# Experts of a mixture layer with the weights as stationary operand, and one slot less

## The chip, the cores and the metric

The kernel runs on one core of one Trainium2 chip. It is one program of about 45,000 executed instructions. The metric is the device time in microseconds of one execution. A core has five engines: TensorE (PE: products, with PEld its weight loads and PEldq its sequencer, which works through registers, waits and branches and passes the products on), VectorE (DVE), ScalarE (ACT), GpSimd (POOL) and SyncE (SP), which issues DMAs. In a product one operand is stationary: it is loaded into the array first, 128 columns of it here. The other one moves through the array column by column.

## The reference, cut to what matters

Four sublayers follow each other: cross attention, a feed-forward layer with quantised products, a second cross attention, and a mixture of experts. The change touches the last one alone.

```python
# x: (8, 512, 512), 4096 tokens of 512 numbers; 8 experts, 2 for each token; MOE_DIM = 1024
x_flat = x.reshape(b * s, d)                       # the normed x
topk_logits, topk_idx = jax.lax.top_k(x_flat @ moe_router, 2)
topk_weights = softmax(topk_logits)
sort_idx = argsort(topk_idx.reshape(tokens * 2))   # the 8192 pairs by expert
x_sort = x_flat[token_ids_sort]
w13_out = ragged_dot(x_sort, moe_w13, group_sizes)         # (8192, 2048)
gate, up = split(w13_out, [1024], axis=-1)
hidden = silu(gate) * up
out_dispatch = ragged_dot(hidden, moe_w2, group_sizes)     # (8192, 512)
out_flat = zeros.at[token_ids_sort].add(out_dispatch * w_sort[:, None])
```

## The kernel before, in words

The stages run one after another, each a block with a barrier at its end: context, attention 0, feed-forward, attention 1, routing, experts, combine. Routing sorts the 8192 pairs of token and expert by expert into `sorted_x`, in slots of 128 rows; each slot belongs to one expert, and the number of its expert stands in `plan.expert`. There are 64 + 8 = 72 slots (`SLOTS`).

The function `experts` works through the slots. The weights of two experts at a time are held in the on-chip memory, `weights13` (gate and up, 512 x 2048) and `weights2` (1024 x 512), each as a high and a low part in bf16. A product of two numbers is made of three bf16 products (`PRODUCTS`: high with high, high with low, low with high). The stages of a slot are:

- SP loads 128 rows of `sorted_x` into `x_rows`.
- `flip_x` (line 1779): TensorE transposes them in 8 pieces, ScalarE copies the result to `x_t`.
- `half_products` (line 1789): gate and up, 512 columns of each in one half. The tokens of `x_t` are stationary, the weights move, 512 columns to a product. The result has a token in each row. Each half has 2 parts x 4 k x 3 = 24 products. Which of the two weight buffers is read depends on `expert % 2`, a value in a register; in the listing of the instructions a row `ISA` before a product is the arithmetic on registers that works out such an address.
- ScalarE applies Silu to gate (line 1849), VectorE multiplies with up (1876) and splits the product `mid` into a high and a low part, `mid_parts` (1880, 1882).
- `flip_mid` (line 1799): TensorE transposes the parts of a half in 8 pieces, and VectorE copies them to `mid_t` (1889), since the next product needs the features of `mid` in the rows.
- `output` (line 1809): `mid_t` is stationary, `weights2` moves: 8 x 3 = 24 products of 512 columns into one bank, `out`. ScalarE copies it to `y_rows` (1855), SP stores it to `sorted_y`.

Each engine goes through the slots by itself in the order written in its own `slot` function, and semaphores hold them together. `slots` writes out the first two and the last two slots and has a loop over pairs of slots between. On TensorE the order within slot s is: read the number of the expert, first half of s, transposes of the x rows of s + 1, transposes of the second half of s - 1, second half of s, output of s - 1, transposes of the first half of s. GpSimd loads the weights of the expert after next and splits them as soon as the output of the last slot of an expert is there (`pool.wait_ge(out_ready, end)`).

Of the kernel before, what the change touches and what calls it, by code (L numbers as in the profile page):

```python
# [26 lines left out]
P = 128  # L27
# [1302 lines left out]
SLOTS = (2 * B * S) // P + EXPERTS  # L1330
# [329 lines left out]
def experts(nc, core, plan, w, sorted_x, sorted_y):  # L1660
# [5 lines left out]
    with ExitStack() as stack:  # L1666
# [7 lines left out]
        mid_parts = sb("mid_parts", [P, 2, 2, 512], BF16)  # L1674
        mid_t = sb("mid_t", [P, 2, MC, P], BF16)
# [9 lines left out]
        split = sem("split"); mid_high = sem("mid_high"); mid_low = sem("mid_low")  # L1685
        x_in = [sem(f"x_in{i}") for i in range(2)]
# [4 lines left out]
        mid_flipped = sem("mid_flipped"); mid_copied = sem("mid_copied")  # L1691
# [5 lines left out]
        def slots(engine, slot):  # L1697
# [6 lines left out]
            slot(SLOTS - 2, 0, False, False)  # L1704
            slot(SLOTS - 1, 1, False, True)
# [49 lines left out]
        def _(sp):  # L1755
# [14 lines left out]
            for u in range(2):  # L1770
                sp.wait_ge(y_out[u], 16 * PAIRS)

        @block.tensor
        def _(pe):
# [20 lines left out]
            def flip_mid(s, half):  # L1795
                pe.wait_ge(mid_low, 2 * s + half + 1)
                at_least(pe, mid_copied, 2 * s + half - 1)
                for j in range(MC):
                    last = nc.tensor.transpose(mid_flip[half][:, j * P:(j + 1) * P],  # L1799
                                               mid_parts[:, half, j // 4, j % 4 * P:(j % 4 + 1) * P],  # L1800
                                               core.ident_bf[:, :])
# [206 lines left out]
```

## Time and profile before

| | |
|---|---|
| runs | 3473.69, 3482.69, 3483.56 us |
| median | 3482.69 us |
| span of the profiled execution | 3475.7 us |
| experts stage in it | 2152 to 3377 us |
| slots, time of one in the loop | 72, 16.88 us |

The profile page sums the busy time of each engine and cuts the span into 40 slices of 87 us. Each digit is the busy share of a slice in tenths. The trace answers closer questions: stretches, groups by source line, and instructions in order of time. A matmul is recorded from its start until its result is written, longer than the distance to the next one, since they are pipelined. Distances are therefore read from starts.

### The profile page before, as it was taken

The page shows a single profiled execution, that of the slowest core. Times are in us where ns is not written, and L with a number is a line of the kernel's source. Part 1 is how long each engine was busy: PE and PEld are TensorE (multiplying, and loading weights), DVE is VectorE, ACT ScalarE, POOL GpSimd, SP SyncE. Part 2 cuts the span into 40 slices and gives each one's busy share as a digit, 9 for nine tenths or more (in the row PEclk, how much of TensorE's full clock was granted, in tenths as well). Part 3 has the DMA queues.
Part 4 walks back from the last instruction along what each step waited for, and adds up shares of the span by engine and source line. Part 5 has one row for each costly group of instructions (what it writes and reads, how often), then busy time and mean ns, then how long its engine had stood idle before and what let it go on. Part 6 is the DMA issues. An engine that isn't in the chain of part 4 may idle for free. (4 is left out here: it accounts for less than half of the span.)

```text
span 3475.7 us, 44833 instructions
## 1 busy us (share of the span) xinstructions
PE 2708.8 (78%) x14170; PEld 1390.6 (40%) x14171; DVE 1980.7 (57%) x2814; ACT 1157.9 (33%) x1751; POOL 934.7 (27%) x739
## 2 busy tenths in 40 slices
PE   7578888446656647888888831999999999999980
PEld 4245555212222214444555310454444445444440
DVE  3287777689999996666666463223333332333225
ACT  2133333266656535555555332111111111111110
POOL 0001010046756751111111025002233350550007
PEclk9789999678877878999999775999999999999995
DMA  9800000100000010000000145001222230320018
GB/s 383 130 30 6 11 5 8 49 0 1 1 0 0 1 51 9 8 8 11 7 7 8 37 145 179 31 30 61 72 69 82 86 107 30 103 91 30 30 43 275
DMA packets 146005, 194.13 MB, mean 56 GB/s; under 512 B 85073, under 2 KB 85073, under 8 KB 145417
## 3 DMA queue, kind: packets, MB, share of 16 engines
q1 hardware_dynamic: 120569, 102.96, 10.6%
q0 software_dynamic: 25360, 90.21, 7.5%
q8 instruction: 41, 0.67, 0.1%
q14 instruction: 35, 0.29, 0.0%
HBM read 122.65 MB, written 70.48 MB: 56 GB/s over the span
## 5 line engine op out<-in xcount | busy, mean ns | idle before, releaser
L1789 PE MATMUL e_gate_up<-weights,e_x_t 128*128 x3456 | 771.5, 380 | 1.4 <-ACT e_x_t L1843 1.4
L1789 PEld LDWEIGHTS e_gate_up<-weights,e_x_t 128*128 128x128 bf16 x3456 | 332.6, 98 | 377.0 <-issue 4.3
L1876 DVE TENSOR_TENSOR e_mid<-e_gate,e_gate_up 128x512 f32<-128x512 f32 x144 | 99.0, 687 | 644.0 <-ACT e_gate L1849 644.0
L1809 PE MATMUL e_out<-weights,e_mid_t 128*128 x1728 | 384.7, 379 | 1.1 <-DVE e_mid_t L1889 1.1
L1849 ACT ACTIVATE e_gate<-e_gate_up 128x512 f32<-128x512 f32 x144 | 86.0, 597 | 684.0 <-PE e_gate_up L1789 684.0
L546 PE MATMUL a_turn<-a_wo,a_mixed_t 128*128 128x512 bf16 (+1 forms) x1024 | 284.2, 434 | 2.3 <-DVE a_mixed_t L804 1.7
L1035 PE MATMUL f_product<-f_xq_t,f_w 128*128 128x512 bf16 x512 | 168.2, 468 | 118.7 <-DVE f_padded L1236 89.9
L1809 PEld LDWEIGHTS e_out<-weights,e_mid_t 128*128 128x128 bf16 x1728 | 169.1, 98 | 204.8 <-issue 1.2
L479 POOL TENSOR_TENSOR a_probs<-a_e,a_probs 128x616 bf16<-128x616 f32 x64 | 85.6, 1353 | 545.1 <-ACT a_probs L713 545.1
L989 POOL TENSOR_TENSOR f_shared<-f_shared 128x512 f32<-128x512 f32 x128 | 180.8, 1413 | 171.0 <-DVE f_shared L1268 171.0
L978 POOL TENSOR_TENSOR hidden<-hidden,f_up_row 128x512 f32<-128x512 f32 x128 | 199.1, 1565 | 88.2 <-ACT f_up_row L1181 88.2
L637 ACT ACTIVATE a_probs_t<-a_flip 77x512 f32<-77x512 f32 (+1 forms) x256 | 191.2, 800 | 46.6 <-PE a_flip L495 46.5
L1053 PE MATMUL f_out<-f_w,f_shared 128*128 128x512 bf16 x512 | 155.5, 438 | 60.8 <-DVE f_shared L1275 60.0
L1889 DVE COPY e_mid_t<-e_mid_flip 128x1024 bf16<-128x1024 bf16 x144 | 98.9, 687 | 180.9 <-PE e_mid_flip L1799 180.9
L546 PEld LDWEIGHTS a_turn<-a_wo,a_mixed_t 128*128 128x128 bf16 (+1 forms) x1024 | 123.1, 121 | 144.8 <-issue 55.9
L1739 POOL TENSOR_TENSOR e_token<-e_token 1x1 f32<-1x1 f32 x6 | 1.1, 183 | 657.5 <-PE e_out L1809 657.5
L659 ACT ACTIVATE a_e<-a_e 128x616 f32<-128x616 f32 x128 | 91.6, 716 | 234.8 <-DVE a_e L783 165.7
L532 PE MATMUL a_turn<-a_probs_t,a_values 77*128 77x512 f32 (+1 forms) x448 | 164.4, 514 | 1.8 <-ACT a_probs_t L637 1.8
L1855 ACT ACTIVATE e_y_rows<-e_out 128x512 f32<-128x512 f32 x72 | 43.0, 597 | 340.3 <-PE e_out L1809 340.3
L1746 POOL TENSOR_TENSOR weights<-raw_weights,weights 128x1024 bf16<-128x1024 f32 x72 | 154.1, 2140 | 6.1
L1921 POOL DMA_INDIRECT o_y<-sorted_y,plan_rows x64 | 67.8, 1059 | 283.9 <-PEq L1907 264.7
L1268 DVE SCALAR_TENSOR_TENSOR f_shared<-f_padded,f_conv_w,f_shared 128x512 f32<-128x512 f32 x128 | 139.6, 1091 | 3.2 <-ACT f_shared L1136 3.2
(234 smaller groups left out, 4485.5 us busy)
## 6 DMA issues: line engine op xcount, KB each, us to landing
raw_weights<-in_w POOLq DMA_DIRECT2D x72, 512.0 KB, 4.0
sorted_x<-c_zero_row POOLq DMA_DIRECT2D x1, 18432.0 KB
e_x_rows<-sorted_x SPq DMA_DIRECT2D x72, 256.0 KB, 2.7
sorted_y<-e_y_rows SPq DMA_DIRECT2D x72, 256.0 KB, 2.0
raw_weights<-in_w SPq DMA_DIRECT2D x24, 512.0 KB, 4.1
x<-in_x SPq DMA_DIRECT2D x4, 2048.0 KB, 49.1
out<-x SPq DMA_DIRECT2D x32, 256.0 KB, 4.2
hidden<-in_w_t SPq DMA_DIRECT2D x1, 4096.0 KB, 13.6
```

The lines of the kernel that those rows point to most:

```text
L532: last = nc.tensor.matmul(mix_banks[c % 2], values[:, a, c * HPC + j, :], probs_t[0:KEYS, d, c * HPC + j, :], start=(j == 0 and a == d == ...
L546: last = nc.tensor.matmul(turn[i % 2][:, :], mixed_t[:, a, c, i * P:(i + 1) * P], wo[:, d, c, :], start=(c == 0 and a == d == 0), stop=(c ...
L637: nc.scalar.activation(probs_t[0:KEYS, :, QT * q:QT * (q + 1), i * P:(i + 1) * P], typed(flip[q % 2][:, :])[0:KEYS, :].rearrange("p (a h n ...
L978: nc.gpsimd.tensor_tensor(hidden[:, j, :], hidden[:, j, :], up2_row[:, :], ALU.mult).then_inc(scaled_up, 1)
L989: nc.gpsimd.tensor_tensor(y[:, j % BUF, :], y[:, j % BUF, :], side[:, j % BUF, :], ALU.add).then_inc(right_added, 1)
L1035: last = nc.tensor.matmul(product[j % 2][:, :], w1[:, k, j % HC * P:(j % HC + 1) * P], xq_t[:, parity, k, :], start=(k == 0), stop=(k == K ...
L1053: last = nc.tensor.matmul(out[i][:, :], hq[:, j, i * P:(i + 1) * P], w2[:, j, :], start=(j == 0), stop=(j == HC - 1))
L1268: nc.vector.scalar_tensor_tensor(y[:, j % BUF, :], padded[:, j % BUF, 0:S], conv_w[:, j, 0:1], y[:, j % BUF, :], ALU.mult, ALU.add).then_i ...
L1746: nc.gpsimd.tensor_tensor(parts[1], plan.raw[:, n % 2, :], parts[0], ALU.subtract).then_inc(split, 1)
L1789: last = nc.tensor.matmul(gate_up[half][:, part, :], x_t[:, u, a, k, :], plan.weights13[:, bass.ds(expert % 2, 1), b, k, col:col + 512], s ...
L1809: last = nc.tensor.matmul(out[:, :], mid_t[:, a, j, :], plan.weights2[:, bass.ds(expert % 2, 1), b, j, :], start=(j == 0 and a == b == 0), ...
L1876: nc.vector.tensor_tensor(mid[:, half, :], gate[:, half, :], gate_up[half][:, 1, :], ALU.mult).then_inc(mid_made, 1)
```

## The change

Gate and up are computed the other way round. The weights are stationary, in pieces of 128 x 128, and the 128 tokens of `x_t` move. The result has a feature of `mid` in each row and a token in each column, which is the shape that `output` needs as its stationary operand. So `flip_mid`, `mid_copy`, `mid_parts` and the banks `mid_flip` are gone, and VectorE writes the high and low parts straight to `mid_t`, which becomes double. `out` has two banks. There are 71 slots, one fewer: groups of 8 experts whose sizes sum to 8192 never need more than 64 + 7 slots of 128. The unrolled end has three slots, and the loop makes 33 rounds where it made 34.

```diff
-SLOTS = (2 * B * S) // P + EXPERTS
+SLOTS = (2 * B * S) // P + EXPERTS - 1
...
-        mid_parts = sb("mid_parts", [P, 2, 2, 512], BF16)
-        mid_t = sb("mid_t", [P, 2, MC, P], BF16)
+        mid_t = sb("mid_t", [P, 2, 2, MC, P], BF16)
...
-        mid_flip = [pb(f"mid_flip{h}", [P, 2 * MC // 2 * P], BF16) for h in range(2)]
-        out = pb("out", [P, 512])
+        out = [pb(f"out{u}", [P, 512]) for u in range(2)]
...
-                for part in range(2):
-                    col = part * MID + half * 512
-                    for k in range(KD):
-                        for a, b in PRODUCTS:
-                            last = nc.tensor.matmul(gate_up[half][:, part, :], x_t[:, u, a, k, :],
-                                                    plan.weights13[:, bass.ds(expert % 2, 1), b, k, col:col + 512],
-                                                    start=(k == 0 and a == b == 0),
-                                                    stop=(k == KD - 1 and a == 1))
+                for j in range(HC):
+                    for part in range(2):
+                        col = part * MID + (half * HC + j) * P
+                        for k in range(KD):
+                            for a, b in PRODUCTS:
+                                last = nc.tensor.matmul(gate_up[half][:, part, j * P:(j + 1) * P],
+                                                        plan.weights13[:, bass.ds(expert % 2, 1), b, k, col:col + P],
+                                                        x_t[:, u, a, k, :],
+                                                        start=(k == 0 and a == b == 0),
+                                                        stop=(k == KD - 1 and a == 1))
...
-            def flip_mid(s, half):
-                pe.wait_ge(mid_low, 2 * s + half + 1)
-                at_least(pe, mid_copied, 2 * s + half - 1)
-                for j in range(MC):
-                    last = nc.tensor.transpose(mid_flip[half][:, j * P:(j + 1) * P],
...
-                pe.wait_ge(mid_copied, 2 * s + 2)
-                at_least(pe, out_copied, s)
+                pe.wait_ge(mid_low, 2 * s + 2)
+                at_least(pe, out_copied, s - 1)
...
                 half_products(s, u, 0, expert)
                 if not last:
                     flip_x(s + 1, 1 - u)
-                if not first:
-                    flip_mid(s - 1, 1)
                 half_products(s, u, 1, expert)
                 if not first:
-                    output(s - 1, expert_of(s - 1))
-                flip_mid(s, 0)
+                    output(s - 1, 1 - u, expert_of(s - 1))
```

The order of TensorE's instructions, first around the middle of slot s in the loop of before: the end of the first half, the transposes of x and of the product, the start of the second half. A name in square brackets is a semaphore that is waited for.

```order
L1789 MATMUL e_gate_up<-weights,e_x_t 128x512
L1789 ISA
L1789 MATMUL e_gate_up<-weights,e_x_t 128x512 x2
L1776 ISA
L1779 MATMUL e_flip<-ident_bf,e_x_rows 128x128 [waits e_x_copied,e_x_in1]
L1779 MATMUL e_flip<-ident_bf,e_x_rows 128x128 x7
L1796 ISA
L1799 MATMUL e_mid_flip<-ident_bf,e_mid_parts 128x128 [waits e_mid_copied,e_mid_low]
L1799 MATMUL e_mid_flip<-ident_bf,e_mid_parts 128x128 x7
L1789 ISA [waits e_mid_made]
```

And the same place in the changed kernel, on TensorE, at the end of the first half of a slot:

```order
L1790 MATMUL e_gate_up<-e_x_t,weights 128x128
L1790 ISA
L1790 MATMUL e_gate_up<-e_x_t,weights 128x128 x2
L1776 ISA
L1779 MATMUL e_flip<-ident_bf,e_x_rows 128x128 [waits e_x_copied,e_x_in1]
L1779 MATMUL e_flip<-ident_bf,e_x_rows 128x128 x7
L1790 ISA [waits e_mid_made]
```

The transposes of the product are gone from between the halves, the products have 128 columns in place of 512, and their pattern with the `ISA` rows is the same: one `ISA`, one product, one `ISA`, two products. A half had 8 such groups of three products; it has 32 now.

The end of a slot on TensorE in the changed kernel, where the second half goes over into the output of the slot before:

```order
L1790 MATMUL e_gate_up<-e_x_t,weights 128x128 x2
L1808 ISA
L1808 TENSOR_LOAD plan_expert
L1808 ISA x2
L1798 ISA
L57 REGISTER_ALU [waits e_mid_low]
L1802 ISA [waits e_out_copied]
L1802 MATMUL e_out<-weights,e_mid_t 128x512
L1802 ISA
L1802 MATMUL e_out<-weights,e_mid_t 128x512 x2
```

The output waits for VectorE's split (`mid_low`) where it waited for the copy `mid_copied`; its 24 products and 16 `ISA` rows are as before, and no transposes follow it.

## Rows read from the trace of the kernel before

**Rows 1.** The page: busy us, share and instructions; 40 slices with TensorE's clock.

```profile
PE 2708.8 (78%) x14170; PEld 1390.6 (40%) x14171; DVE 1980.7 (57%) x2814; ACT 1157.9 (33%) x1751; POOL 934.7 (27%) x739
...
PE   7578888446656647888888831999999999999980
...
PEclk9789999678877878999999775999999999999995
```

**Rows 2.** Stretches: from:to, length, busy us (instructions) by engine, clock, DMA.

```profile
core 0: us, PE busy (x) PEld busy (x) DVE busy (x) ACT busy (x) POOL busy (x), PEclk, DMA share, GB/s
2200.00:2400.00 200.00, 200.00 (x1142) 99.43 (x1141) 58.72 (x96) 31.87 (x47) 0.00 (x0) 1.00 0.09 32
```

**Rows 3.** TensorE in order of time, one slot: start us, us, engine, line, what.

```profile
2300.32 5.34 PE L1809 MATMUL e_out<-weights,e_mid_t 128*128 x24
2305.50 0.61 PE L1799 MATMUL e_mid_flip<-ident_bf,e_mid_parts 128*128 128x128 bf16 x8
2305.94 5.34 PE L1789 MATMUL e_gate_up<-weights,e_x_t 128*128 x24
2311.12 0.61 PE L1779 MATMUL e_flip<-ident_bf,e_x_rows 128*128 128x128 bf16 x8
2311.57 0.61 PE L1799 MATMUL e_mid_flip<-ident_bf,e_mid_parts 128*128 128x128 bf16 x8
2312.02 5.34 PE L1789 MATMUL e_gate_up<-weights,e_x_t 128*128 x24
2317.20 1.03 PE L1809 MATMUL e_out<-weights,e_mid_t 128*128 x4
```

**Rows 4.** Line 1789, whole trace: ns min/median/max, first and last start.

```profile
L1789 PEld LDWEIGHTS e_gate_up<-weights,e_x_t x3456: 97/98/147, 2157.6 to 3363.1; 128*128 128x128 bf16 x192
L1789 PEldq FUSED_REGOPS  x2304: 46/46/118, 2157.4 to 3359.2; - x192
```

**Rows 5.** Line 1789 in the stretch 2446.05 to 2447.95.

```profile
L1789 PEldq FUSED_REGOPS  x16: 46/46/46, 2446.1 to 2447.9; - x16
```

**Rows 6.** Line 1789 from 3233.46 to 3235.48, and from 3234.19 to 3235.07.

```profile
L1789 PEldq FUSED_REGOPS  x16: 46/46/99, 3233.5 to 3235.5; - x16
L1789 PEldq FUSED_REGOPS  x8: 46/46/46, 3234.2 to 3235.1; - x8
```

**Rows 7.** Sequencer: slot head, second reading, loop end, before the x transposes.

```profile
L1815 PEldq FUSED_REGOPS  x2: 42/96/151, 2303.4 to 2303.8; - x2
L1815 PEldq TENSOR_LOAD <-plan_expert x1: 299/299/299, 2303.5 to 2303.5; - x1
L1789 PEldq FUSED_REGOPS  x2: 51/78/104, 2304.4 to 2304.6; - x2
...
L1815 PEldq TENSOR_LOAD <-plan_expert x1: 307/307/307, 2313.3 to 2313.3; - x1
L1809 PEldq FUSED_REGOPS  x1: 104/104/104, 2314.6 to 2314.6; - x1
2313.91 0.68 DVE L1889 COPY e_mid_t<-e_mid_flip 128x1024 bf16<-128x1024 bf16 x1
...
L1701 PEldq ALU_OP  x1: 32/32/32, 3232.0 to 3232.0; - x1
L1701 PEldq COMPARE_BRANCH  x1: 222/222/222, 3232.1 to 3232.1; - x1
L1776 PEldq FUSED_REGOPS  x1: 83/83/83, 2307.3 to 2307.3; - x1
```

**Rows 8.** Line 1809 from 2299.5 to 2306: end of one output group.

```profile
L1809 PE MATMUL e_out<-weights,e_mid_t x24: 379/379/379, 2300.3 to 2305.3; 128*128 x24
L1809 PEldq FUSED_REGOPS  x6: 46/46/46, 2299.7 to 2301.2; - x6
```

**Rows 9.** Second attention: a stretch, and 16 transposes in it.

```profile
1516.60:1523.40 6.80, 5.87 (x73) 4.38 (x71) 3.97 (x7) 4.50 (x6) 0.07 (x1) 1.00 0.13 22
1518.25 1.06 PE L495 MATMUL a_flip<-ident_bf,a_probs 128*77 128x128 bf16 x16
```

**Rows 10.** VectorE's copy by group (busy, mean ns, idle before); waits from 2150 to 3300.

```profile
L1889 DVE COPY e_mid_t<-e_mid_flip 128x1024 bf16<-128x1024 bf16 x144 | 98.9, 687 | 180.9 <-PE e_mid_flip L1799 180.9
...
POOL e_token L1739 <- PE e_out L1809: 657.5, 6, 252.8
...
DVE e_mid L1876 <- ACT e_gate L1849: 609.6, 136, 28.0
```

**Rows 11.** DMA queue of instructions from 1525 to 1850 us; the stores of a slot.

```profile
q8 instruction: 1, 0.02, 0.0%
...
sorted_y<-e_y_rows SPq DMA_DIRECT2D x72, 256.0 KB, 2.0
```

More of the change, by code:

```diff
@@ L1703, in slots @@
                 slot(2 * pair + 1, 1, False, False)
-            slot(SLOTS - 2, 0, False, False)
-            slot(SLOTS - 1, 1, False, True)
+            slot(SLOTS - 3, 0, False, False)
+            slot(SLOTS - 2, 1, False, False)
+            slot(SLOTS - 1, 0, False, True)
         @block.gpsimd
@@ L1793, in half_products @@
-                last.then_inc(halves_ready, 1)
-            def flip_mid(s, half):
-                pe.wait_ge(mid_low, 2 * s + half + 1)
-                at_least(pe, mid_copied, 2 * s + half - 1)
-                for j in range(MC):
-                    last = nc.tensor.transpose(mid_flip[half][:, j * P:(j + 1) * P],
-                                               mid_parts[:, half, j // 4, j % 4 * P:(j % 4 + 1) * P],
-                                               core.ident_bf[:, :])
-                last.then_inc(mid_flipped, 1)
@@ L1804, in output @@
-            def output(s, expert):
-                pe.wait_ge(mid_copied, 2 * s + 2)
-                at_least(pe, out_copied, s)
+                for j in range(HC):
[8 more added lines that the diff above has]
+                                                        stop=(k == KD - 1 and a == 1))
@@ L1807, in output @@
+                last.then_inc(halves_ready, 1)
+            def output(s, u, expert):
+                pe.wait_ge(mid_low, 2 * s + 2)
+                at_least(pe, out_copied, s - 1)
                 for j in range(MC):
                     for a, b in PRODUCTS:
-                        last = nc.tensor.matmul(out[:, :], mid_t[:, a, j, :],
+                        last = nc.tensor.matmul(out[u][:, :], mid_t[:, u, a, j, :],
                                                 plan.weights2[:, bass.ds(expert % 2, 1), b, j, :],
@@ L1854, in out_copy @@
                     act.wait_ge(y_out[u], 16 * (s // 2))
-                nc.scalar.activation(y_rows[:, u, :], out[:, :], ACT.Copy).then_inc(out_copied, 1)
+                nc.scalar.activation(y_rows[:, u, :], out[u][:, :], ACT.Copy).then_inc(out_copied, 1)
             x_copy(0, 0)
@@ L1867, in _, with multiply @@
             slots(act, slot)
-            out_copy(SLOTS - 1, 1)
+            out_copy(SLOTS - 1, (SLOTS - 1) % 2)
         @block.vector
         def _(dve):
-            def multiply(s, half):
+            def multiply(s, u, half):
                 n = 2 * s + half
                 dve.wait_ge(gate_made, n + 1)
-                at_least(dve, mid_low, n - 1)
                 nc.vector.tensor_tensor(mid[:, half, :], gate[:, half, :], gate_up[half][:, 1, :], ALU.mult
@@ L1878, in multiply @@
                 dve.wait_ge(mid_made, n + 1)
-                at_least(dve, mid_flipped, n - 1)
-                nc.vector.tensor_copy(mid_parts[:, half, 0, :], mid[:, half, :]).then_inc(mid_high, 1)
+                if half == 0:
+                    at_least(dve, out_ready, s - 1)
+                parts = [mid_t[:, u, a, half * HC:(half + 1) * HC, :].rearrange("p j n -> p (j n)") for a in range(2)]
+                nc.vector.tensor_copy(parts[0], mid[:, half, :]).then_inc(mid_high, 1)
                 dve.wait_ge(mid_high, n + 1)
-                nc.vector.tensor_tensor(mid_parts[:, half, 1, :], mid[:, half, :], mid_parts[:, half, 0, :],
-                                        ALU.subtract).then_inc(mid_low, 1)
-            def mid_copy(s, half):
-                dve.wait_ge(mid_flipped, 2 * s + half + 1)
-                if half == 0:
-                    at_least(dve, out_ready, s)
-                nc.vector.tensor_copy(mid_t[:, :, half * MC // 2:(half + 1) * MC // 2, :],
-                                      mid_flip[half][:, :].rearrange("p (a j n) -> p a j n", a=2, j=MC // 2)
-                                      ).then_inc(mid_copied, 1)
-            def slot(s, u, first, last):
-                multiply(s, 0)
-                if not first:
-                    mid_copy(s - 1, 1)
-                multiply(s, 1)
-                mid_copy(s, 0)
+                nc.vector.tensor_tensor(parts[1], mid[:, half, :], parts[0], ALU.subtract).then_inc(mid_low, 1)
+            def slot(s, u, first, last):
+                multiply(s, u, 0)
+                multiply(s, u, 1)
             slots(dve, slot)
-            mid_copy(SLOTS - 1, 1)
 def combine(nc, core, plan, sorted_y, out):
```

8 lines of the change are left out of this document (4 added, 4 removed).

## The prediction

> **What bounds the kernel now.** I read the page first (shares by engine and the 40 slices), then the stretches, then one slot in order of time, then the rows of the sequencer. [Rows 1] show TensorE as the busiest engine, with a solid row of nines and a full granted clock from the 25th slice on: that is the experts stage. [Rows 2] sharpen it: in 200 us there, TensorE is busy for 200.00 us, at clock 1.00 (the 2.4 GHz level). Nothing else is near. So in this stage time is made of TensorE's own instructions and nothing is hidden behind anything.
>
> [Rows 3] are one slot. Twenty-four products of 512 columns start at 2305.94 and the next group starts at 2311.12: 5.18 us, 0.216 us each. The two groups for gate and up and the one for the output have 72 such products, 15.54 us. Transposes come in eights, 0.445 us from one group's start to the next (2311.12, 2311.57, 2312.02), 0.056 us each; there are 24, 1.34 us. The sum is 16.88 us, and the slot does take 16.88 us (2300.32 to 2317.20). 72 slots are 1215.4 us of the 3475.7 us span.
>
> **What the change removes from the array.** The 16 transposes of the product go, 16 x 0.056 = 0.89 us a slot. Their weight loads overlap the products, as all loads do here. Gate and up become 192 products of 128 columns in place of 48 of 512. The columns are the same, but the fixed part is paid 192 times. The nearest row for a short product with its own full load is a run of 16 transposes, 1.06 us with a last one of 0.22 us [rows 9]: (1.06 - 0.22) / 15 = 0.056 us. So 192 x 0.056 = 10.75 us against 10.36 us now. With 5.18 us for the output and 0.45 us for the x transposes the array needs 16.38 us a slot, 0.50 us less than now. If the array were all, the change would gain 71 x 0.50 and a slot of 16.88, some 50 us.
>
> **What the change adds to the sequencer, the term that decides.** Every product of this stage has one operand at an address that depends on the expert of the slot, and in the order it is preceded by an ISA row that works this address out: two such rows for three products. The trace calls them FUSED_REGOPS and shows them on TensorE's sequencer (PEldq), 2304 of them for 3456 products [rows 4], 32 a slot. The change writes the same two rows around every three products, but a product is now a quarter as long: 64 groups of three, 128 such rows a slot, and 16 for the output as before. Before, 16 rows were needed in 5.18 us and nobody saw them. What does one cost when the sequencer is not held up by a full queue? [Rows 5] hold a whole group, 16 of them from 2446.05 to 2447.95, in which 24 products were also passed on: 1.89 us for 15 steps, 0.126 us each, though each is recorded with only 46 ns. The best stretch has 8 in 0.88 us, 7 steps of 0.124 us, and a slow one 16 in 2.01 us, 0.133 us [rows 6]. So three products, which the array can do in 0.168 us, take the sequencer two steps, 0.25 us. The ratio of rows to products is the same in the change as in these stretches, so the pitch carries over: I take 0.127 us, nearest to the whole group, with ends 0.124 and 0.133.
>
> The sequencer's time for a slot of the changed kernel, all worked out from rows of before:
> - 144 address rows x 0.127 = 18.29 us; the first of each of the three groups costs about 0.06 us more (104 ns recorded in place of 46 [rows 7]), 0.18 us.
> - the head of the slot, reading the expert from memory and checking it: from the load's first row at 2303.4 to the first address row at 2304.4 [rows 7], 1.06 us with the digits behind; the second reading, before the output, is 0.3 us of load, 0.15, 0.02 and the gaps. It took 1.3 us (2313.3 to 2314.6 [rows 7]), but there it stood for the VectorE copy out of the transposes, which ends at 2314.59 and goes away. I take 1.0 us, bounds 0.7 and 1.3.
> - the loop's end once in two slots, rows of 32, 222 and 59 ns with gaps, 0.53 us [rows 7], so 0.27 us a slot; the address and wait ahead of the x transposes 0.25 us (83 and 51 ns recorded, with gaps as above).
>
> Together 21.05 us, against 16.38 us for the array. A part of the longer one is lost to the full queue: in [rows 8] the last six address rows of an output group end at 2301.2 while its last product starts at 2305.3, 19 products of 0.216 us later; two products follow that row, so the sequencer can be at most about 17 products ahead. During the output's 5.18 us it needs only 3.2 us for output and head, is 9 ahead, fills the rest in about 1 us and stands for some 0.8 us in which it could have done 60% more than the array takes. I take 0.4 us, bounds 0 and 0.8. The slot is then **21.45 us**, 4.57 us more than now.
>
> The Trainium skill, "TensorE: Matmul & The Clock Gate", section "Back-to-back issue gap", speaks against this change in another way: it gives about 81 ns for each pair of a load and a 128-column product in a sustained stream, on the array itself. The row of transposes above shows 56 ns, so the trace does not agree; by that rule the slot would be an estimated 192 x 0.081 + 5.63 = 21.2 us, which is 290 us more in all, near my sum for another reason.
>
> **What else moves, at no cost.** VectorE's 144 copies of 0.69 us go, but it was waiting for most of the stage [rows 10]; its cast and subtraction write the same elements to another tile. ScalarE reads the same 128x512 shape. The double output bank takes away a wait that was already met. GpSimd waited for the outputs of an expert, up to 252.8 us [rows 10], and with longer slots waits longer. Removing a slot is in the count of 71; its store and load were hidden. The last slot loses the wait of 1.08 us for the copy, and the first loses a group of outputs that is cheap for the sequencer; together under 3 us, left at nothing.
>
> **The sum.** 71 x 21.45 - 72 x 16.88 = 1523.0 - 1215.4 = +307.6 us. The profiled execution is 3475.7 us; the median of the runs, 3482.7 us, is 7.0 us above it, which I keep. 3475.7 + 307.6 + 7.0 = **3790 us**.
>
> **Rivals.**
> - *Not slower: the address rows are no limit.* The price of 0.124 us might be one that only the recorded execution pays, or that falls when the queue drains. Against it: never less than 0.124 us in the rows read, and the profiled span is no longer than the runs without a profile, although other stages hang on sequencers too. The point is 72 x 16.88 / 71 = 17.12 us a slot, that is (17.12 - 2.76) / 144 = 0.100 us for a row. With no limit at all the slot is 16.4 to 16.7 us and the time 3483 - 1215 + 71 x 16.55 = 3443 us. Chance 0.06, and 0.01 for a result within 0.3%.
> - *The weight loads set the pace.* A load is recorded with 98 ns [rows 4]; now its address is the one that is computed, while all loads before had fixed ones. If loads no longer overlap each other, a pair takes 98 ns, the slot 192 x 0.098 + 5.63 = 24.4 us, the time 3483 - 1215 + 1735 = 4003 us. For it: no row of before has such a load. Against: 56 ns between loads of the same size. Chance 0.04.
> - *Fetching instructions.* The loop of two slots grows from 509 to 1212 instructions. If they no longer stay on the chip, each round fetches them again. The loop of the second attention has 1052, and in 325 us of it a single block came over q8 [rows 11]: it stays. If not, there are five blocks in each of 33 rounds. A small transfer takes 2.0 us from issue to landing here [rows 11]; with half of that hidden it is 170 us more, 3960 us. Chance 0.04. The Trainium skill, "Advanced Engine Details and Errata", section "ISA Cache", gives TensorE 128 KB; at 64 bytes each the new loop is an estimated 76 KB, so by it this rival falls.
> - *The clock.* With gaps between its products TensorE may be granted 1.2 GHz. Then 128 columns take 0.107 us and 512 take 0.427, the slot 31.6 us, and the time rises by 1028 us to 4511 us. Against: a stretch of 6.8 us with 73 short products (11 a microsecond; the change has 12) was at 1.00 [rows 9]. Chance 0.03.
>
> **Chances and range.** The forecast has 0.80; what is left, 0.02, lies above it. Its own ends: pitch 0.124, second reading 0.7 and no loss give 20.3 us, +227, 3710 us; pitch 0.133, 1.3 and 0.8 us give 23.0 us, +418, but not all at once, so 22.6 us, +389, 3872 us. That holds 0.80, and no more than 0.2 is outside; I give 3710 to 3875. Faster by over 0.3% 0.06, within 0.3% (about what a measurement of this kernel can tell from no change) 0.01, slower 0.93.
>
> **What the profile after would show.** 128 address rows a slot at 0.124 to 0.13 us from start to start nearly all the time, gate and up half groups of about 8.1 us in place of 5.2, TensorE's loads idle with "issue" named as the cause, clock 1.00, and slots of 21 to 22 us. Wrong steps would show as: address rows closer than 0.1 us (the first rival); pairs at an even 98 ns with the address rows far ahead (the second); blocks on q8 all through the stage and pauses at the loop's end (the third); PEclk at 0.5 (the fourth). The forecast fails above all if the pitch of an address row is other with short products than in the stretches of before.

## The result and the profile after

| | before | changed kernel |
|---|---|---|
| median of the runs | 3483.12 us (3473.69 to 3483.95) | 3788.42 us (3786.12 to 3792.84) |
| span of the profiled execution | 3475.7 us | 3785.9 us |
| slots, time of one | 72, 16.88 us | 71, 21.41 us in the mean |

The changed kernel is slower: ratio 1.0888, 95% interval 1.0870 to 1.0906. The forecast was 3790 us in a range of 3710 to 3875.

The page of the changed kernel, busy time by engine, then TensorE, its weight loads and its clock in 40 slices, which are 95 us long now. Beside [rows 1]:

```profile
PE 2962.1 (78%) x23162; PEld 1886.6 (50%) x23163; DVE 1906.5 (50%) x2664; ACT 1162.6 (31%) x1747; POOL 934.1 (25%) x739
...
PE   7578887355666578889885199999999999999990
PEld 4245554122222245544442177777777777777760
...
PEclk9789999678878789999987599999999999999995
```

The page still shows nines for TensorE and a full clock. Read alone, it says "TensorE is busy", as before. A product is recorded until its result is written, 219 ns here, and within a half nearly every one starts at most 170 ns after the one before, so the gaps between their starts do not appear as idle time. The stretch that answers to [rows 2] shows a little more (columns as there):

```profile
2200.00:2400.00 200.00, 192.58 (x2085) 143.41 (x2082) 32.65 (x55) 25.94 (x37) 0.00 (x0) 1.00 0.08 25
```

2085 products in 200 us are 9.3 slots of 21.4 us; without gaps in the starts it would be 1.3 times as many, since a slot is some 16.4 us where the array alone sets it (below). The clock is 1.00, the 2.4 GHz level, as before. What a slot is made of is seen in order of time (beside [rows 3]: start us, us, engine, line, what, and in brackets the idle time before it):

```profile
2404.42 8.02 PE L1790 MATMUL e_gate_up<-e_x_t,weights 128*128 128x128 bf16 x96
2413.22 5.35 PE L1802 MATMUL e_out<-weights,e_mid_t 128*128 x24 [0.77 <-issue]
...
2418.41 6.94 PE L1790 MATMUL e_gate_up<-e_x_t,weights 128*128 128x128 bf16 x96
2425.34 0.61 PE L1779 MATMUL e_flip<-ident_bf,e_x_rows 128*128 128x128 bf16 x8
2425.78 8.02 PE L1790 MATMUL e_gate_up<-e_x_t,weights 128*128 128x128 bf16 x96
2434.67 5.35 PE L1802 MATMUL e_out<-weights,e_mid_t 128*128 x24 [0.87 <-issue]
2439.86 6.94 PE L1790 MATMUL e_gate_up<-e_x_t,weights 128*128 128x128 bf16 x96
```

From output to output (2413.22 to 2434.67) are 21.45 us. The output itself is as before (24 products, 5.19 us from start to start). The second half takes 8.0 us, where the array alone would need 5.4; then the array stands 0.77 to 0.87 us with "issue" as the cause, while the sequencer reads the number of the expert; the first half takes 6.9 us, since its first products were queued during the output. The sequencer's own rows in the half from 2404 to 2412 (line 1790; count, ns min/median/max, first and last start), beside [rows 5]:

```profile
L1790 PEldq FUSED_REGOPS  x64: 46/46/46, 2404.0 to 2412.1; - x64
```

64 address rows in 8.1 us, 0.128 us from one to the next: the same pitch as in the stretches of before where nothing held the sequencer up. It has no pause in this stretch; the array waits for it after every three products. Of the address rows of line 1790 in the stage, the most frequent distance is 124 ns.

### The profile page after: what moved, and what is told of

It reads as the page before. It is cut to its first block and busy times, and to the rows that moved or that the text cites. A ratio compares the mean times of both kernels' runs of the same rounds, so it can differ in the third digit from the quotient of the medians.

```text
span 3785.9 us, 68849 instructions
## 1 busy us (share of the span) xinstructions
PE 2962.1 (78%) x23162; PEld 1886.6 (50%) x23163; DVE 1906.5 (50%) x2664; ACT 1162.6 (31%) x1747; POOL 934.1 (25%) x739
## 5 line engine op out<-in xcount | busy, mean ns | idle before, releaser
L1790 PE MATMUL e_gate_up<-e_x_t,weights 128*128 128x128 bf16 x13632 | 1069.4, 223 | 2.4 <-ACT e_x_t L1832 1.4
L1790 PEld LDWEIGHTS e_gate_up<-e_x_t,weights 128*128 x13632 | 902.8, 97 | 171.4 <-issue 4.4
L1035 PEld LDWEIGHTS f_product<-f_xq_t,f_w 128*128 128x128 bf16 x512 | 54.7, 114 | 211.3 <-DVE f_padded L1236 110.0
L1872 DVE TENSOR_TENSOR e_mid_t<-e_mid,e_mid_t 128x512 bf16<-128x512 f32 x142 | 141.6, 998 | 4.9
```

The lines of the kernel that those rows point to most:

```text
L1035: last = nc.tensor.matmul(product[j % 2][:, :], w1[:, k, j % HC * P:(j % HC + 1) * P], xq_t[:, parity, k, :], start=(k == 0), stop=(k == K ...
L1790: last = nc.tensor.matmul(gate_up[half][:, part, j * P:(j + 1) * P], plan.weights13[:, bass.ds(expert % 2, 1), b, k, col:col + P], x_t[:, ...
L1872: nc.vector.tensor_tensor(parts[1], mid[:, half, :], parts[0], ALU.subtract).then_inc(mid_low, 1)
```

## The experiments

The theory is that the sequencer's address rows set the pace. The experiments change their number and leave the array's work as it is, then put branches in their place, and last try to take the gain that remains. The kernel before took between 3475 and 3477 us on the chips of these runs, and the ratios are against that.

**One, two and three address rows.** One kernel has one address row for three products in gate and up, where the change has two; one has three; and one has none. The one with three also reads the number of the expert once more in each slot.

```diff
 # one row (and the low part of the weights isn't read)
-plan.weights13[:, bass.ds(expert % 2, 1), b, k, col:col + P],
+plan.weights13[:, bass.ds(expert % 2, 1), 0, k, col:col + P],
 # three rows: the number of the expert is read a second time, into another register
-plan.weights13[:, bass.ds(expert % 2, 1), b, k, col:col + P],
+plan.weights13[:, bass.ds((again if a else expert) % 2, 1), b, k, col:col + P],
 # none: a fixed stationary operand
-plan.weights13[:, bass.ds(expert % 2, 1), b, k, col:col + P],
+core.ident_bf[:, :],
```

> The changed kernel, but gate and up read the high part of the weights in all three products, so one address row serves three products: 64 in place of 128 a slot (it leaves out the low part of the weights). The products and their loads, with a computed address in each load, are as many as in the change. If the address rows on the sequencer set the pace, they need 80 x 0.127 + 2.8 = 13.0 us a slot and the array with 16.4 to 16.9 us takes over: 3483 - 1215 + 71 x 16.65 = 3450 us, between 3430 and 3475. If the pairs of a load with a computed address and a 128-column product take 84 ns on the array, nothing changes: 3788 us.

> The changed kernel with the expert read twice at the head of a slot, and the second value used for the third product of each three, so that every product of gate and up has an address row of its own: 192 a slot in place of 128; products, loads and result are the same. If address rows set the pace, a slot grows by 64 x 0.127 us and a reading of about 0.8 us, 21.4 to 30.3 us: 3788 + 71 x 8.9 = 4420 us, between 4350 and 4480. If the array's pairs set it at 84 ns, the rows have 0.12 us and still fall short of it only at the reading: a third row costs at most 192 x 0.124 = 23.8 us in all, and without a price on the sequencer the time stays within 60 us of 3788 us.

> The changed kernel with a fixed tile, the identity, as the stationary operand of gate and up (it leaves out the weights of gate and up), so no address is worked out for them: no address rows, 192 loads with a fixed address, the same moving side. If address rows set the pace, the array's 16.4 us a slot and what shows of the readings are left, 16.5 to 16.9 us: 3450 us, between 3435 and 3475. If short products with the tokens moving cannot go closer than 84 ns for a reason in the array, 3788 us. Between this and the run with one row: equal times say that a computed address in a load costs the array nothing.

Measured, one run each: 3438.0 us with one row, 4412.6 us with three, 3431.7 us with a fixed operand. The steps between one, two and three rows are 350 us and more, while the kernel before varied by 10 us beside them; the 6 us between one row and none are within that. The same place of a slot in the three, in that order (columns as above):

```profile
2409.15 5.52 PE L1790 MATMUL e_gate_up<-e_x_t,weights 128*128 128x128 bf16 x96
2414.56 5.35 PE L1802 MATMUL e_out<-weights,e_mid_t 128*128 x24
```

```profile
2408.23 12.06 PE L1790 MATMUL e_gate_up<-e_x_t,weights 128*128 128x128 bf16 x96
2421.18 3.19 PE L1802 MATMUL e_out<-weights,e_mid_t 128*128 x14 [0.89 <-issue]
```

```profile
2404.67 5.52 PE L1790 MATMUL e_gate_up<-e_x_t,ident_bf 128*128 128x128 bf16 x96
2410.05 5.35 PE L1802 MATMUL e_out<-weights,e_mid_t 128*128 x24
```

Half a slot of gate and up takes 5.4 us, 8.0 us and 12 us with one, two and three rows for three products. One row costs 0.124 us and three products cost the array 0.168 us, so one row is hidden and two or three are not: 96 rows x 0.124 = 11.9 us. The slots are 16.5 us in the median, 21.4 and 30.2 us in the mean. The price of a row doesn't hang on what is passed on between two of them: with three rows, so one product to a row, the most frequent distance is 0.124 us too, and in the kernel with one row 310 distances, each with three products in it, are 0.124 or 0.125 us. In the kernel with three rows the granted clock was 0.97 in the stage; at the lower level a product of 128 columns takes 0.107 us (below), still less than a row. The kernel with one row still loads its weights from an address in a register, 128 x 128 every 56 ns, and its half slot is as long as that of the kernel with a fixed operand, 5.4 us. This settles two rivals: a load at a computed address costs the array nothing more, and its recorded 97 ns are no pace. The 56 ns also decide against the figure of some 81 ns for a pair of a load and a 128-column product in a sustained stream (the Trainium skill, "TensorE: Matmul & The Clock Gate", "Back-to-back issue gap"): here are 96 such pairs in a row at 56 ns.

**The slot alone.** The kernel before with 71 slots, and nothing else changed.

```diff
-SLOTS = (2 * B * S) // P + EXPERTS
+SLOTS = (2 * B * S) // P + EXPERTS - 1
```

> The kernel before with 71 slots in place of 72 and nothing else: one part of the change alone. Both theories: one slot of 16.88 us less, 3483 - 17 = 3466 us (ratio 0.995). If the empty slot was hidden anyway, no change.

Measured: 3457.68 us (3453.27 to 3460.35), ratio 0.9952, 95% interval 0.9935 to 0.9968. A slot still takes 16.88 us, and its share of the time goes. This part of the change is a gain of 0.5%, on its own the best version of this study. The rest of the change thus costs 71 x (21.41 - 16.88) = 322 us, not 305.

**Branches in place of address rows.** Each half is written out twice, for weight buffer 0 and 1 with fixed addresses, and the sequencer branches on the parity of the expert. The second of these kernels also reads the expert of the slot before at the head of the slot.

```diff
+                with pe.If(expert % 2 == 0):
+                    products(0)          # the loops of half_products, with
+                with pe.Else():          # plan.weights13[:, 0, ...] or [:, 1, ...]
+                    products(1)
```

> The changed kernel with gate and up written out twice, once for each of the two places of the weights, and a branch on expert % 2 at the head of each half. All addresses of gate and up are then fixed, nothing is left out of the computation. If the address rows were the whole cost, the slot falls to the array's 16.4 us and little more: the queue of 17 short pairs covers about 0.95 us, which hides the second reading as in the run with one row, and a branch costs about 0.3 us of the sequencer. 16.5 to 16.9 us a slot, 3450 us (3440 to 3470), ratio to before 0.990. The loop on TensorE grows to about 1,900 instructions. If these do not stay on the chip, or a branch over 192 products waits for instructions, each of four branches in a round costs 1 us or more, the slot is 18 us and above, and the time 3550 us or more.

> As the run with branches, but the expert of the slot before is read at the head of the slot, behind the 512-column products of an output, and not between the last short product and the output. If the reading shows in the array's time only where short products stand ahead of it, this gains up to 0.3 us a slot on the run with branches, 3435 to 3450 us; if a full queue already hides it there, the two are equal within 0.1 us a slot (7 us).

Measured: 3635.48 us (ratio 1.0481, 95% interval 1.0448 to 1.0515) and 3606.58 us (1.0386, 1.0358 to 1.0413). Both are far above the 3450 us that the array would need, for a new reason. The first of the two in order of time, and its instruction queue from 2300 to 3300 us (packets, MB, share):

```profile
2414.20 8.31 PE L1792 MATMUL e_gate_up<-e_x_t,weights 128*128 128x128 bf16 x96 [3.53 <-issue]
2422.35 0.61 PE L1779 MATMUL e_flip<-ident_bf,e_x_rows 128*128 128x128 bf16 x8
2422.80 5.52 PE L1792 MATMUL e_gate_up<-e_x_t,weights 128*128 128x128 bf16 x96
2428.28 5.35 PE L1809 MATMUL e_out<-weights,e_mid_t 128*128 x24
2433.47 5.52 PE L1792 MATMUL e_gate_up<-e_x_t,weights 128*128 128x128 bf16 x96
...
q8 instruction: 230, 3.77, 1.6%
```

Where the sequencer is not held up, a half takes 5.4 us and a slot 16.4 to 16.8: without address rows the array is the limit again. But every second slot, the one with the loop's end in it, is 21.7 and 21.4 us in the median of the two kernels, and up to 25.5. The loop has 1734 TensorE instructions, and 230 blocks of 16 KB are fetched in 1000 us, some 9 for each round; the changed kernel, with 1212, fetches none over q8 in the same stretch. The branch at the end of the loop in the second of the two kernels, of all 33 rounds:

```profile
L1700 PEldq COMPARE_BRANCH  x33: 83/3696/5126, 2217.2 to 3445.3; - x33
```

3.7 us in the median, against 0.222 us in [rows 7]. So the third rival of the prediction exists; it only doesn't strike the changed kernel. The fourth shows here too. Toward the end of the pause of 3.53 us and behind it the granted clock was at its lower level, 1.2 GHz (stretch, busy us by engine and clock as in [rows 2]):

```profile
2413.25:2420.08 6.83, 5.88 (x56) 5.88 (x57) 0.00 (x0) 0.00 (x0) 0.00 (x0) 0.50 0.17 45
```

The first 55 products of that half start every 0.107 us, the others every 0.056 us: that is why it takes 8.2 us and not 5.4. Over 1000 us the clock is 0.96 in both kernels, where the changed kernel has 1.00. Fetches and clock together make the slot 19.5 and 19.2 us in the mean, against 16.5 us without; most of it is the pauses.

The second kernel also answers the question for which it was made. In the slots without the loop's end it takes 16.39 us in the median, the first 16.74: the reading shows where it stands between the last short product and the output, and costs 0.35 us there.

**How much the full queue takes.** The products of the output, which cost the sequencer little, are spread among those of the second half, so that the queue is never full for 5 us. The address rows stay the same in number; the reading of the number of the slot before moves ahead of the second half.

```diff
                 for part in range(2):
                     ...                      # 12 products of gate or up
+                    if between:
+                        between(2 * j + part)  # 3 products of the output of s - 1
```

> The changed kernel with the eight threes of output products of the slot before put between the 128-column groups of the second half, in place of behind it; every instruction is the same otherwise. It tests the term for the full queue: the 512-column products no longer come in a block that fills the queue and holds the sequencer up. If 0.4 us a slot were lost to that, the slot is 21.0 us and the time 3788 - 28 = 3760 us. If the sequencer never stood (its rows alone sum to 21.4), it stays at 3788 us within 7 us.

Measured: 3741.54 us, ratio 1.0785 (1.0750 to 1.0819), 47 us less than the changed kernel. A slot, from transposes to transposes:

```profile
2403.64 0.61 PE L1779 MATMUL e_flip<-ident_bf,e_x_rows 128*128 128x128 bf16 x8
...
2424.44 0.61 PE L1779 MATMUL e_flip<-ident_bf,e_x_rows 128*128 128x128 bf16 x8
```

The slot falls from 21.41 to 20.99 us in the mean, 0.42 us: the loss that the prediction put at 0.4. In 71 slots that is 30 us, and the expert stages of the two profiled executions differ by 30.1 us. The other 17 us are not the change's: the stage begins 17 us earlier in this execution, with the same instructions ahead of it. Without a loss the stage would have stayed as long as it was.

**Half of each.** The first half of a slot as before (tokens stationary, transposes, copy), the second as in the change, with the output spread in it: 96 address rows a slot in place of 144.

```diff
-                half_products(s, u, 0, expert)
+                tokens_held(s, u, expert)      # 24 products of 512 columns, as before
...
                 half_products(s, u, 1, expert, lambda j: output(s - 1, 1 - u, before, [j]))
+                flip_mid(s)
```

> The first half of a slot is computed as in the kernel before (tokens stationary, 512 columns to a product, its parts transposed and copied), the second half as in the changed kernel, with the products of the output of the slot before spread between its groups; 71 slots. The sequencer then has 16 address rows for the first half and 64 + 16 for the second with the output, 96 in all, 96 x 0.124 = 11.9 us, with heads and branches about 14.5 us, under the array's. If the address rows are the only limit, the array sets the slot: 16.88 less one group of 8 transposes (0.45) plus 0.2, since 96 short products take 96 x 0.056 = 5.38 us where 24 long ones took 5.18: 16.63 us. Against the kernel before with 71 slots (3457.7 measured) this is 69 x 0.25 = 17 us less, about 3440 us. The rival, that short products interleaved with long ones lose time of their own in the array (a switch of shapes or banks at each of 8 places a slot), would show as a slot over 16.9 us and a time of 3460 us or more.

Measured: 3469.29 us, ratio 0.9983 (0.9973 to 0.9992): 0.2% under the kernel before, but slower than 71 slots alone. Neither theory had it right. Of the slots without the loop's end 24 of 31 are 16.61 us, what the array needs, the others up to 17.5 us; those with the loop's end are some 17.3 us. A seam between two slots, with the loop's end:

```profile
2626.25 0.83 PE L1814 MATMUL e_gate_up<-e_x_t,weights 128*128 128x128 bf16 x12
2626.92 0.81 PE L1830 MATMUL e_out<-weights,e_mid_t 128*128 x3
2627.57 0.83 PE L1814 MATMUL e_gate_up<-e_x_t,weights 128*128 128x128 bf16 x12
2628.24 0.81 PE L1830 MATMUL e_out<-weights,e_mid_t 128*128 x3
2628.88 0.61 PE L1802 MATMUL e_mid_flip<-ident_bf,e_mid_parts 128*128 128x128 bf16 x8
2629.95 5.35 PE L1792 MATMUL e_gate_up<-weights,e_x_t 128*128 x24 [0.46 <-DVE e_mid L1896]
```

The groups of 12 and 3 products follow each other every 1.32 us, which is the array's 12 x 0.056 + 3 x 0.216, so mixing short and long products costs nothing. But their ten address rows take the sequencer 1.27 us; it comes out of the second half barely ahead of the array, and then has the loop's end and the head of the slot before it, in its own rows from 2628.347 to 2629.793. VectorE is named as the releaser here, but its multiplication for this wait was done at 2619.1; it was the sequencer.

The sequencer also started the second half with less of a lead than the queue allows. Ahead of the x transposes it waits for the rows that SyncE loads, and in each of 63 slots in the middle of the stage its next row starts 0.06 us after that load has landed, often with 11 to 14 pairs of load and product ahead of the array and not 17 or 18. In the changed kernel and in the interleaved one this happens in no slot. What the mixed kernel would take with the rows there in time was not tried.

**One half branching.** As in the interleaved kernel, but the first half branches and the second keeps its address rows. The loop has 1476 instructions.

```diff
+                if half == 1:
+                    products(bass.ds(expert % 2, 1))
+                else:
+                    with pe.If(expert % 2 == 0):
+                        products(0)
+                    with pe.Else():
+                        products(1)
```

> The changed kernel with the output of the slot before spread between the groups of the second half, as in the interleaved run, and with the first half written out twice, once for each weight buffer, with a branch on the parity of the expert in place of its 64 address rows. The loop over pairs has 1476 TensorE instructions, between the 1212 of the changed kernel, which brought no fetches of instructions, and the 1734 of the branching kernels, which fetched some 230 blocks in 1000 us. 80 address rows a slot are left, 80 x 0.124 = 9.9 us, with heads and branches some 12.5 us, under the 16.0 us that the array needs. If 1476 instructions stay resident, the slot is 16.1 to 16.5 us and the time 3405 to 3435 us. If the loop is fetched anew in each round, the slot is 18.5 us or more in the mean, the time over 3560 us, and the instruction queue shows over 100 blocks in 1000 us.

Measured: 3515.11 us, ratio 1.0110 (1.0093 to 1.0127). One part of the expectation holds: no blocks over q8, and a loop's end like before, so 1476 instructions stay and 1734 don't. The other part falls: a slot is 17.69 us, not 16.1 to 16.5, and the 16.0 us that I gave the array were too few, since no slot of any kernel with these products took less than 16.35. The place of the heads again:

```profile
2616.67 0.81 PE L1815 MATMUL e_out<-weights,e_mid_t 128*128 x3
2618.27 5.53 PE L1792 MATMUL e_gate_up<-e_x_t,weights 128*128 128x128 bf16 x96 [0.79 <-DVE e_mid L1880]
2623.64 0.61 PE L1779 MATMUL e_flip<-ident_bf,e_x_rows 128*128 128x128 bf16 x8
2624.09 1.15 PE L1792 MATMUL e_gate_up<-e_x_t,weights 128*128 128x128 bf16 x12
2625.34 0.82 PE L1815 MATMUL e_out<-weights,e_mid_t 128*128 x3
```

The sequencer's loop end and head go from 2616.560 to 2618.044, and the array, with nothing queued, stands 0.95 us. Another 0.5 to 0.6 us goes at the start of the second half, behind the reading of the number of the slot before: its first 12 products take 1.25 us until the next group, in place of 0.67. I had summed the sequencer's rows over the slot and compared the sum with the array's. A sum under the array's time says that it can keep up on average, not that it is ahead where its long steps are.

**The heads at another place.** If so, the heads should stand where the queue is fullest, behind the long products. TensorE's order is turned: readings and loop end ahead of the second half, in the mixed kernel and in the one with one half branching. With it the transposes of the x rows come a slot earlier, those of s + 2 in slot s.

```diff
             def slot(s, u, first, last):
+                # before, expert and after: read here, three after the loop's end, else one
                 half_products(s, u, 1, expert, lambda j: output(s - 1, 1 - u, before, [j]))
                 flip_mid(s)
+                first_half(s + 1, 1 - u, after)
+                flip_x(s + 2, u)
```

> The mixed kernel (first half with the tokens stationary, second half with the weights stationary and the output of the slot before spread in it, 71 slots), with TensorE's order turned: the numbers of the experts of three slots are read, and the loop branches, ahead of the second half, right behind the 24 long products of a first half and 8 transposes, in place of ahead of the first half, where the sequencer came out of the short products with no lead (1.0 us from the first row of the head to the first address row, at 2611.107 to 2612.143 in the mixed kernel, and slots of 17.2 to 17.9 us in every second place where the others took 16.61). 96 address rows a slot stay. If the lost lead at the head is what kept the mixed kernel from 16.61 us a slot, all slots are 16.61 to 16.7 us: 69 x 0.4 = 28 us less than 3469.3, about 3441 us. If the address rows, interleaved with other products, cost more than 0.124 us each, the slot stays near 17.0 and the time near 3469 us.

> The kernel with one half branching (both halves with the weights stationary, 1476 instructions in the loop, measured 3515.1 us and 17.6 us a slot), with the same turn of the order: the readings of the experts' numbers stand ahead of the second half. The queue ahead of the array there holds some 17 pairs of short products, 17 x 0.056 = 0.95 us, against 1.0 to 2.2 us of head, so part of the head stays exposed: 0.1 to 1.2 us over the 16.47 us that the array needs, 16.6 to 17.5 us a slot, 3440 to 3505 us, with 3465 us as the middle. A time under 3440 us would say that the queue hides the head whole; one of 3515 us, that the place of the head is nothing.

Measured: 3526.65 us, ratio 1.0146 (1.0129 to 1.0163), and 3587.05 us, 1.0323 (1.0305 to 1.0340). Both are slower than their counterparts, and both expectations missed. The mixed kernel, at a slot without the loop's end and at one with it:

```profile
2601.94 0.61 PE L1782 MATMUL e_flip<-ident_bf,e_x_rows 128*128 128x128 bf16 x8
2602.39 0.83 PE L1814 MATMUL e_gate_up<-e_x_t,weights 128*128 128x128 bf16 x12
...
2618.73 0.62 PE L1782 MATMUL e_flip<-ident_bf,e_x_rows 128*128 128x128 bf16 x8
2621.69 1.19 PE L1814 MATMUL e_gate_up<-e_x_t,weights 128*128 128x128 bf16 x12 [2.34 <-issue]
```

```profile
L1837 PEldq TENSOR_LOAD <-plan_expert x3: 296/299/302, 2619.2 to 2620.7; - x3
L1703 PEldq ALU_OP  x1: 32/32/32, 2618.7 to 2618.7; - x1
```

Where one number is read (2602), the head is hidden whole and the slot is 16.6 to 16.8 us for the most part: this half of the idea holds. At the loop's end it fails twice over. The slot needs three readings there, since no register is carried over, so the head is 2.78 us (2618.745 to 2621.525) in place of 1.4. And the lead was short: 8 pairs of load and product in the slot shown, the transposes, worth 0.45 us, where 17 pairs with nine long ones among them would have been worth 2.4 us. The cause is the load of the x rows, needed a slot earlier in this order:

```profile
2614.57 0.34 SPq L1768 DMA_DIRECT2D e_x_rows<-sorted_x  x1
...
2618.72 0.45 PEld L1782 LDWEIGHTS e_flip<-ident_bf,e_x_rows 128*128 128x128 bf16 x8 [0.50 <-DMA e_x_rows<-sorted_x]
```

It landed at 2618.68, and the sequencer, which stood in the wait ahead of the transposes, goes on at 2618.745. This holds in 63 of 63 slots in the middle of the stage; where the load lands earlier the sequencer is 12 to 14 pairs ahead, as at 2600.970. Slots with the loop's end take 18.5 us in the median, the one shown 20.6. Address rows in the middle of other products keep their price (ten in 1.27 us), so that theory is out. The theory of the head wasn't tested cleanly, since the turn brought a longer head and a new wait with it.

In the kernel with one half branching the lead was the expected one, mostly 16 to 18 pairs. Slots without the loop's end are 16.9 us, those with it 20.5: there the array is idle for 1.85 us ahead of 2607.98, behind the same three readings, and the granted clock falls to its lower level next to it. It is 0.96 in the stage, against 1.00 in the counterpart.

## Why the prediction was right

Its time came out within 2 us, and its terms can be checked one by one. The mechanism is the one that was forecast; that the last 5 us fit as well is luck. The expert stage grew by 306.1 us (forecast 307.6), the stages beside it were 4.1 us longer in this execution, for which there was no term, and the median of the runs is 2.5 us above the profiled span where 7.0 had been kept.

- *What bounds the stage.* Right: the array before; the sequencer after. The three kernels with one, two and three rows show it from both sides, with slots of 16.5, 21.4 and 30.2 us.
- *The array's need, 16.38 us.* The shortest slots of the kernel with one row, and of the second one with branches, are 16.35 us. The median of 16.47 us has some 0.1 us more between the last short product and the output, where the reading stands (0.08 to 0.22 us in place of 0.056), and the mean of 16.57 us has waits of up to 1.0 us for the x rows. The short products cost 0.056 us as taken from the transposes in [rows 9].
- *An address row, 0.127 us.* Measured 0.128 us over a half (64 in 8.1 us), most often 0.124. This term was 18.3 of 21.45 us, and it was read from three lines of the kernel before, in which it cost nothing [rows 5, 6]. The prediction let it carry over because as many products stand between two rows as before. The runs show that this wasn't needed: with one product or with three to a row the distance is 0.124 us as well.
- *The second reading, 1.0 us.* From the last address row of the half to the first of the output are 1.00 us (2412.058 to 2413.057, rows of the sequencer), of which 0.12 is the pitch: 0.87 us. *The head*, 1.06 us: 0.95 and 1.03 us in two slots. *The loop's end*, 0.53 us: 0.49 us.
- *The loss to the full queue, 0.4 us.* Measured twice: in the gaps of the sequencer's rows at the start of a first half, 0.24 us in one slot and some 0.66 us in the next, and as 0.42 us less in the interleaved kernel. Its 20.99 us are also the 21.05 us of the sum without a loss.
- *The slot, 21.45 us*: 21.41 us. *The sum*, +307.6 us on the profiled execution: 3785.9 - 3475.7 = +310.2 us. 71 x 21.41 - 72 x 16.88 are +304.7 of them. The first and last slots bring 1.4 us, "under 3 us" as said. The other 4.1 us are outside the stage: it began 4.8 us later in this execution, and what follows it was 0.6 us shorter.
- *The rivals.* No limit by address rows: refuted by the pitch, and by the kernel with one row, which is 350 us faster. Loads setting the pace: refuted by 56 ns with computed addresses. Instruction fetches: not here, but at 1734 instructions. The estimate by a cache of 128 KB (the Trainium skill, "Advanced Engine Details and Errata", "ISA Cache") was right for this kernel's 76 KB and the 92 KB of 1476 instructions, at 64 bytes each; by it 1734 instructions, 108 KB, should stay as well, and they don't. The clock: 1.00 in the stage, so this too is out here; the pauses of 0.77 to 0.87 us didn't lower it, one of 3.53 us in the branching kernel did.

What the prediction didn't set apart is that the change holds two parts of opposite sign: one slot less is -0.5%, the other orientation +9.4% over that.

## What to carry to other kernels

Count what the sequencer must do for each product, not only what the array must: an operand at an address worked out from a register costs a row of 0.124 us for each new address, whatever its recorded 46 ns say (the third product of three has no row here, since it uses the first one's address again). It hides behind 512-column products (0.216 us each) and not behind 128-column ones (0.056 us). Before products are made smaller, look for the densest stretch of such rows in the trace of the kernel as it is and take their pitch from start to start; that a sequencer can keep up on average is not enough, since its long steps (a reading of 0.9 us, a loop's end of 0.5) need a queue that is full where they stand, and a wait for a load just ahead of them keeps it from filling.

## What the runs showed of the hardware

- A weight load from a computed address, 128 x 128, follows the one before by 56 ns, as with a fixed address.
- A row that works out an address takes TensorE's sequencer 0.124 us from start to start, with one, one and a half or three products passed on to a row.
- Groups of short and long products alternate in the array with no loss: 12 of 128 and 3 of 512 columns every 1.32 us.
- A loop of 1476 TensorE instructions with forward branches brought no fetches, one of 1734 brought 230 blocks of 16 KB in 1000 us and 3.7 us in the median at its end. It has twice as many branches as well, so whether the size or their number decides is not shown. The branches in the middle of the loop of 1734 took 0.24 us in the median and up to 2.7 us in the second of its two kernels, those of the loop of 1476 at most 0.56 us:

```profile
L1799 PEldq COMPARE_BRANCH  x160: 63/243/2697, 2304.6 to 3299.6; - x160
```

- The lead of the sequencer over the array is at most 17 or 18 pairs of load and product, in [rows 8] and in most slots of the kernels with branches in one half; where 7 to 14 were counted in the mixed kernels, the sequencer had been waiting for a load to land.
- The granted clock stayed at 1.00 through pauses of 0.8 us in each slot of the changed kernel. It was 0.97 in the kernel with three rows, with pauses of 0.89 us and a product every 0.124 us in a half, and 0.50 behind a pause of 3.53 us, where 128 columns took 0.107 us in place of 0.056.
